# An LSTM, an attention, a GRU and a mixture of experts on one core: both recurrences in one loop, the GRU 29 steps behind

## The chip, the core and the metric

The kernel runs on one core of a Trainium2 chip. The metric is the device time of one execution in microseconds; three executions of the kernel before took 735.74 us in the median (731.89 to 736.39). The engines are TensorE (PE, with PEld for its loads of the stationary operand), VectorE (DVE), ScalarE (ACT), GpSimd (POOL) and SyncE (SP). Each works through its own instructions in order and waits for the others at semaphores.

## What is computed

x has 16 sequences (b) of 128 steps (t) with 128 features (d), all in float32. Four stages follow each other:

```python
# LSTM over t, its hidden state starting at cond_1024
a = xw_t + prev_h @ Wh
i, f, o = sigmoid(a[:, :128]), sigmoid(a[:, 128:256]), sigmoid(a[:, 256:384]); g = tanh(a[:, 384:])
next_c = f * prev_c + i * g
next_h = o * tanh(next_c)
# causal attention over the LSTM's outputs: 16 heads, keys and values from a latent of 32
x = x + attention(lstm_out)
# GRU over t on the new x
z, r = sigmoid(comb @ Wz + bz), sigmoid(comb @ Wr + br)
h_cand = tanh(concat(x_t, r * h) @ Wh + bh)
h_new = (1.0 - z) * h + z * h_cand
h_next = where(prop, tanh(h_new @ Wp + bp), h_new)      # prop: after each 4th step
# 8 experts of 128 -> 512 -> 128 with gelu, the best 2 of each token weighted
x = x + experts(gru_out)
```

The GRU's step t needs the attention's output for step t, and that needs the LSTM's steps 0 to t. The experts need the GRU's outputs, token by token.

## The kernel before

A step of either recurrence is a chain over three engines. The state is kept as two float16 parts (`hhi` and `hlo`, `ghi` and `glo`), each product with a weight is taken as high by high, high by low and low by high, and sigmoids are written as tanh. An LSTM step: 12 matmuls with 16 columns (8 on `hhi`, 4 on `hlo`), one tanh over the four gates (`lT`, line 729), on DVE `lP`, `oK` and the new cell in `lT`, a tanh of the cell (`lC`, line 733), on DVE `hhi`, `hfull` and `hlo` (lines 906 to 909). A GRU step: 6 such matmuls (or 2 in float32 on `gp` at the first of each four steps), a tanh of both gates (`gT`, line 770), on DVE `gRZ` and `gA`, a float32 matmul on `gRZ`, a tanh (`gC`, line 777), on DVE `gB`, `ghi`, `g8` and `glo`; after each fourth step a matmul with `gWp` and a tanh give `gp`.

The program has three stages, one behind the other.

1. The LSTM in loops over groups of 8 steps (`GS`). Four such groups make a block of `TB` = 32 steps; while the LSTM does block p, the attention of block p-1 is placed between its steps: one unit (one sequence, 16 heads x 32 queries) at steps 1 to 4 of a group for the scores, 3 to 6 for the transposes of the probabilities, 5 to 7 for the values. `keep_warm` puts matmuls of 512 columns on zeros between steps.
2. `last_attention`: the 16 units of the last block, with no recurrence beside them.
3. The GRU in a loop of 16 turns of 8 steps; beside each step one expert on the 128 tokens of the turn before (`layer1`, `layer2`), and the routing (18 small DVE operations, `routing`) spread over the turn.

A float32 matmul appears in the trace as two passes. POOL clears buffers, splits the experts' first weights `w1` into two float16 parts (lines 318 to 321, once, over all 4096 columns), and copies each unit's queries into the block-diagonal `qbd` (line 345).

## Time and profile before

| | |
|---|---|
| time, median of 3 runs | 735.74 us (731.89 to 736.39) |
| the profiled execution, first to last instruction | 731.8 us |
| busy: PE, PEld | 685.2 us (94%), 598.1 us (82%) |
| busy: DVE, ACT, POOL | 461.2 us (63%), 361.6 us (49%), 113.7 us (16%) |
| first LSTM tanh | 28.8 us |
| LSTM's loop | to 330 us |
| last attention | to 381 us |
| GRU's loop | 384 to 711 us |
| rest of the experts | to 731.8 us |

Matmuls are pipelined, so PE counts as busy over more than the time that it takes up: what a matmul costs is the distance from its start to the next one's. A wait printed behind an instruction is idle time of its engine just before it, and the arrow names what ended it.

### The profile page before, as it was taken

The numbers are of one execution on the slowest core, as the hardware profiler recorded it, in microseconds if no ns is written. First come the engines' busy times: TensorE is split into PE (matmuls) and PEld (weight loads), VectorE is DVE, ScalarE is ACT, GpSimd is POOL, SyncE is SP. The second block draws the span as 40 slices with busy tenths as digits, with TensorE's granted clock in tenths as the row PEclk, the third lists the DMA queues.
The fourth block names the chain that finished last, engine by engine and source line by source line (L and its number), as shares of the span: only waits on it lengthen the run. The fifth ranks groups of instructions, "written<-read, shape, count | busy, mean of one in ns | idle before, by whom it ended". The sixth has DMA issues, their size and how long they took to land.

```text
span 731.8 us, 22615 instructions
## 1 busy us (share of the span) xinstructions
PE 685.2 (94%) x7655; PEld 598.1 (82%) x7655; DVE 461.2 (63%) x2374; ACT 361.6 (49%) x1317; POOL 113.7 (16%) x291
## 2 busy tenths in 40 slices
PE   6942999999999999998999999999999999999998
PEld 4521557988888888887989999999999999999996
DVE  2379446676777777876876555655556555565553
ACT  2210224343444444445556666666666666666665
POOL 3068003221322132213310000000000000000000
PEclk8775899898999999999999999999999999999999
DMA  8320000000000000000000000000000000000000
GB/s 196 140 92 0 1 0 3 1 1 0 1 2 0 0 3 2 0 0 1 1 0 6 6 4 0 4 4 4 4 4 4 4 4 3 0 4 4 4 4 8
DMA packets 5669, 9.45 MB, mean 13 GB/s; under 512 B 1884, under 2 KB 4724, under 8 KB 5120
## 3 DMA queue, kind: packets, MB, share of 16 engines
q1 hardware_dynamic: 5008, 6.59, 2.8%
q10 hardware_dynamic: 624, 2.38, 1.3%
q8 instruction: 21, 0.34, 0.2%
q14 instruction: 16, 0.13, 0.1%
HBM read 7.78 MB, written 1.18 MB: 12 GB/s over the span
## 4 chain that ended last, share of the span: by engine, by line
PE 85%; DVE 9%; ACT 2%; issue 2%; DMA 1%; ACTq 0%; POOL 0%; DVEq 0%; POOLq 0%
PE p L363 60%; PE pL L363 21%; PE p L455 4%; DVE hhi L906 4%; DMA Wout<-in_Wout 1%; DVE On L874 1%; DVE lP L897 1%; DVE mx L860 1%; ACT lC L733 1%; ACT lT L729 1%; DVE OT L881 1%; DVE P L865 0%; DVE oK L898 0%; PE p L559 0%; DVE hlo L909 0%
## 5 line engine op out<-in xcount | busy, mean ns | idle before, releaser
L363 PE MATMUL p<-w,hidA 128*128 128x128 f32 x548 | 122.0, 308 | 0.0
L363 PE MATMUL p<-ghi,w1lo 128*128 128x128 f16 x544 | 105.0, 219 | 0.0
L363 PE MATMUL p<-glo,w1hi 128*128 128x128 f16 x544 | 104.8, 219 | 0.0
L363 PE MATMUL p<-ghi,w1hi 128*128 128x128 f16 x544 | 104.8, 218 | 0.0
L761 ACT ACTIVATE hidA<-p,b 128x128 f32<-128x128 f32 x272 | 85.2, 364 | 32.9 <-PE p L363 32.9
L363 PE MATMUL p<-w,hidB 128*128 128x128 f32 x548 | 91.8, 290 | 0.1
L363 PEld LDWEIGHTS p<-w,hidA 128*128 128x128 f32 x548 | 82.7, 192 | 7.8 <-issue 7.7
L761 ACT ACTIVATE hidB<-p,b 128x128 f32<-128x128 f32 x274 | 85.1, 366 | 2.1 <-PE p L363 2.1
L729 ACT ACTIVATE lT<-pL 128x64 f32<-128x64 f32 x128 | 28.5, 223 | 107.7 <-PE pL L363 106.5
L345 POOL COPY qbd<-qT 32x128 f32 x216 | 62.9, 291 | 69.4 <-PE p L363 58.6
L1016 DVE SCALAR_TENSOR_TENSOR gRZ<-gT,g 128x32 f32<-128x32 f32 x128 | 24.7, 193 | 77.4 <-ACT gT L770 74.4
L363 PE MATMUL p<-latT,qbd 128*128 (+1 forms) x512 | 73.3, 288 | 0.0
L363 PEld LDWEIGHTS pL<-hhi,lWhi 128*128 128x128 f16 x512 | 36.4, 98 | 44.0 <-DVE hhi L906 42.4
L363 PEld LDWEIGHTS p<-w,hidB 128*128 128x128 f32 x548 | 72.0, 192 | 0.3 <-ACT hidB L761 0.3
L363 PE MATMUL p<-latN,PTs 32*128 (+4 forms) x512 | 67.7, 276 | 0.8
L363 PE MATMUL pL<-hhi,lWhi 128*128 128x16 f16 x512 | 42.1, 172 | 26.8 <-DVE hhi L906 25.9
L363 PE MATMUL p<-still 128*128 128x512 bf16 x209 | 63.5, 416 | 2.9 <-DVE hlo L819 2.1
L363 PEld LDWEIGHTS p<-latT,qbd 128*128 128x128 f32 x512 | 64.3, 197 | 1.0 <-issue 0.2
L363 PEld LDWEIGHTS p<-latN,PTs 32*128 32x128 f32 (+3 forms) x512 | 61.0, 189 | 2.2 <-issue 1.0
L906 DVE TENSOR_TENSOR hhi<-oK,lC 128x16 f16<-128x16 f32 x128 | 46.3, 362 | 22.5 <-ACT lC L733 21.2
L733 ACT ACTIVATE lC<-lT 128x16 f32<-128x16 f32 x128 | 27.6, 216 | 63.4 <-DVE lT L900 63.1
L363 PEld LDWEIGHTS p<-ghi,w1hi 128*128 128x128 f16 x544 | 55.7, 102 | 1.0
(179 smaller groups left out, 1546.9 us busy)
## 6 DMA issues: line engine op xcount, KB each, us to landing
w<-in_w SPq DMA_DIRECT2D x2, 2048.0 KB, 10.2
out<-acc SPq DMA_DIRECT2D x18, 64.0 KB, 1.5
xT<-in_xT ACTq DMA_DIRECT2D x1, 1024.0 KB, 12.0
...
```

What stands on the lines that cost most here:

```text
L345: pool.tensor_copy(qbd[r, k % 2, :, q, :], qT[r, j % 2, :, ds(b0 + k, 1), :] .rearrange("p g o t -> p g (o t)")).then_inc(qbd_done, 1)
L363: return nc.tensor.matmul(out, lhsT=lhsT, rhs=rhs, start=start, stop=stop, skip_group_check=True)
L455: last = nc.tensor.transpose(pT[:, 128 * g:128 * (g + 1)], P[:, k, g, :], ident[:, :])
L729: A(lT[:, 0:4, :], pL[hf][:, :, s, :], ACT.Tanh, scale=1.0 / SP).then_inc(l_tanh, 1)
L733: A(lC[:, :], lT[:, 4, :], ACT.Tanh, scale=0.5).then_inc(l_tc, 1)
L761: last = A(hid[:, c, :], bank[:, TOK * c:TOK * (c + 1)], ACT.Gelu, bias=b1[:, e, 2 * half + c:2 * half + c + 1], scale=1.0 / SP)
L860: V.tensor_reduce(mx[:, k % 2, :], S_of(k, L), AX.X, ALU.max).then_inc(mx_done, 1)
L874: V.tensor_tensor(On[:, :, :], O_of(k)[:, :, 0:LD], rs[:, :].unsqueeze(2).to_broadcast([128, HG, LD]), ALU.mult).then_inc(on_done, 1)
L881: V.transpose(OT[:, :, k, :], On[:, :, :]).then_inc(ot_done, 1)
L897: V.scalar_tensor_tensor(lP[:, :, :], lT[:, 0:2, :], 1.0, lT[:, 3:5, :], ALU.add, ALU.mult).then_inc(l_mul, 1)
L906: V.tensor_tensor(hhi[:, slot, :], oK[:, :], lC[:, :], ALU.mult).then_inc(l_hi, 1)
L1016: V.scalar_tensor_tensor(gRZ[:, :, :], gT[:, :, :], 1.0, g8[:, at:last + 1:last - at, :], ALU.add, ALU.mult).then_inc(g_rh, 1)
```

## The change

- One straight-line program of 166 steps k takes the place of the three stages. Step k does the LSTM's step t = k (while t < 128), the GRU's step g = k - `LAG` = k - 29, a piece of the attention and a piece of the experts. All loops are gone from the code; waits are for constants.
- The attention works in blocks of `TB` = 16 queries and in units of two sequences (4 x 128 rows of scores in one bank): 8 units a block. In each 16 steps the scores stand at k mod 16 = 2 to 9, the transposes at 3 to 10, the values at 4 to 11, one unit a step. Scores are three float16 products of 16 x (block + 1) keys instead of one float32 product of 128 columns. The projections stand at k mod 16 = 9 and 12, so that the GRU's first step of a block may follow at 13. The last 8 steps of each 16 hold no scores.
- The experts run once for a block of 256 tokens instead of twice for 128. `up_at` puts an expert's two halves (6 matmuls with 256 columns each) at k mod 16 = 13 (4 halves), 14 (2), 15 (4), 0 (2) and 1 (4); `down_at` puts one product of 128 tokens at each step, a block later. The last block's experts follow the last GRU step at k = 157 to 165.
- Routing is done twice in 16 steps (k mod 16 = 5 and 13) in one go: 6 DVE operations (`route_first`) at the end of the step, 2 on POOL (`rank_experts`), one tanh on ACT, 10 on DVE (`route_rest`) at the end of the next step.
- All hidden states and x with the attention added (`x1T`, `hhi`, `hlo`, `g8`, `ghi`, `glo`) stay in full length on chip; `stx` and its copies on POOL are gone.
- Banks: one for the LSTM's gates, one for the GRU's, one for scores and latents (`pS`), one for transposes and values (`pV`), one for queries, projections and routing (`pC`), two for the experts' first products (`pH`), one for their second (`pY`).
- POOL gets more to do: each of 64 units has its queries spread by 4 copies of 32 x 256 float16 (before: 216 copies of 32 x 128 float32 on POOL, 40 on ACT); the latents are split into two float16 parts (2 operations each 8 steps); it scales and splits the GRU's weights, `b2` and `w1`, the last in 12 operations of 1024 columns placed at k = 28 to 31.
- `keep_warm` remains in front of the loop (20) and in steps 0 and 3 to 17 (4 each).

```diff
-TB = 32
+TB = 16
+LAG = 29
+O_S, O_T, O_V = 2, 3, 4
+O_P = (9, 12)
+O_R = (5, 13)
+E_STEP = (0, 0, 1, 2, 2, 3, 4, 4)
...
+            def turn_probs(n):
+                pe.wait_ge(exp_done, n + 1)
+                if n:
+                    pe.wait_ge(on_done, n)
+                for j in range(4):
+                    last = nc.tensor.transpose(pV[:, 128 * j:128 * (j + 1)], P[:, n % 3, j, :], ident[:, :])
+                last.then_inc(pt_mm, 1)
...
+                if n >= 2:
+                    pe.wait_ge(gelu, 2 * (n - 1))
...
+            for k in range(STEPS):
+                t, g = k, k - LAG
+                ups, downs = up_at(k), down_at(k)
+                if 0 <= g < T:
+                    g_step(g)
+                if t < T:
+                    l_step(t)
+                if unit_at(k, O_V) is not None:
+                    values(unit_at(k, O_V))
+                elif half_at(k) is None and ups:
+                    expert_up(*ups.pop(0))
+                if half_at(k) is not None:
+                    project(half_at(k), k)
+                if 0 <= g < T:
+                    g_candidate(g)
+                if k % GS == 0 and GS <= k <= T:
+                    lat_q(k // GS - 1, k)
+                if unit_at(k, O_S) is not None:
+                    scores(unit_at(k, O_S), k)
+                while ups or downs:
+                    if downs:
+                        expert_down(*downs.pop(0))
+                    if ups:
+                        expert_up(*ups.pop(0))
+                if unit_at(k, O_T) is not None:
+                    turn_probs(unit_at(k, O_T))
+                if route_at(k) is not None:
+                    route_x(*route_at(k), k)
...
+                if t % GS == GS - 1 and t + 1 < T:
+                    l_fill((t + 1) // GS)
+                if (g + 1) % GS == 0 and 0 <= g + 1 < T:
+                    g_fill((g + 1) // GS)
+                if 0 <= g < T - 1 and g % 4 == 3:
+                    g_propagate(g)
```

DVE's order in a step is: `gRZ`, `gA`, `lP`, `oK`, `lT`; the normalisation of a unit; `gB`, `ghi`, `g8`; `hhi`, `hfull`; `glo`; `hlo`; then what no recurrence waits for directly: adding x, latents, maximum and subtraction of a unit, `route_rest`, `combine`, `turn_values`, `route_first`. ACT's order is `gT`, `lT`, the unit's exp, the first gelu of a step with ups, `gC`, `lC`, the query copy, the other gelus, the copy of the transposes (`pt_copy`), the routing's tanh, `gp`.

The places in the programs. On PE, in the step behind the LSTM's and GRU's own matmuls, a step of before in the GRU's loop (`w1hi`, `w1lo` are the first expert weights, `hidA` and `hidB` the halves of the hidden layer, `gRZ` the candidate's input):

```order
L363 MATMUL pL<-glo,gWhi 128x16 x2
L363 MATMUL p<-ghi,w1hi 128x128
L363 MATMUL p<-glo,w1hi 128x128
L363 MATMUL p<-ghi,w1lo 128x128
L363 MATMUL p<-ghi,w1hi 128x128
L363 MATMUL p<-glo,w1hi 128x128
L363 MATMUL p<-ghi,w1lo 128x128
L363 MATMUL p<-b2P,ones 128x512
L363 MATMUL p<-w,hidA 128x128
L363 MATMUL pL<-gRZ,gW 128x16
```

And of the change, the step k = 52, from the LSTM's last matmuls to the scores (`PTs` the turned probabilities, `latN` the values, `qbd` the queries):

```order
L444 MATMUL pL<-hlo,lWhi 128x16 x4
L444 MATMUL pV<-latN,PTs 128x33 x4
L444 MATMUL pG<-gRZ,gW 128x16
L444 MATMUL pS<-cmask,ident 128x4x16
L444 MATMUL pS<-lathi,qbd 128x48
L444 MATMUL pS<-latlo,qbd 128x48
```

The same step's end:

```order
L444 MATMUL pY<-b2P,onesP 128x128
L444 MATMUL pY<-w,hid 128x128 x4
L539 MATMUL pV<-ident,P 128x128 x4
L444 MATMUL pG<-ind,biasP 128x512
L444 MATMUL pG<-x1T,gWx 128x128 x3
L444 MATMUL pG<-g,gWp 128x16
L444 MATMUL pG<-g,gW 128x16 x2
```

The values now stand ahead of the candidate's matmul, and the transposes, on which ACT's copy and the next step's values wait, are at the end of the step, behind a product of the experts.

On ACT, around an expert step of before (`hidA`, `hidB`: gelu):

```order
L770 ACTIVATE gT<-pL 128x32
L761 ACTIVATE hidB<-p,b 128x128 x2
L777 ACTIVATE gC<-pL 128x16
L758 REGISTER_ALU
L761 ACTIVATE hidA<-p,b 128x128 x2
```

And of the change, at k = 45, the first step with ups (`th` is the routing's tanh):

```order
L753 ACTIVATE gT<-pG 128x32
L756 ACTIVATE lT<-pL 128x64
L745 ACT_TABLE_LOAD
L745 ACTIVATE hid<-pH,b 128x256 x2
L763 ACTIVATE gC<-pG 128x16
L766 ACTIVATE lC<-lT 128x16
L745 ACTIVATE hid<-pH,b 128x256 x6
L777 ACTIVATE th<-low 128x8
L753 ACTIVATE gT<-pG 128x32
```

A table load now stands between the gates' tanh and the candidate's, and the routing's tanh stands ahead of the next step's `gT`. ACT had 2 table loads in all, one at its first instruction and one ahead of the GRU's loop; it has 14, one at the start and then one ahead of the first gelu and one ahead of the first exp of nearly every 16 steps.

On POOL, the split of `w1` before:

```order
L318 TENSOR_SCALAR w1hi<-w 128x4096
L319 TENSOR_SCALAR w<-w 128x4096
L321 TENSOR_TENSOR w1lo<-w,w1hi 128x4096
```

And of the change, behind the first block's queries:

```order
L413 COPY qbd<-qh 32x8x32 x32
L398 CAST lathi<-latT 128x16x8
L400 TENSOR_TENSOR latlo<-latT,lathi 128x16x8
L390 TENSOR_SCALAR w1hi<-w 128x1024
L391 TENSOR_SCALAR w<-w 128x1024
L393 TENSOR_TENSOR w1lo<-w,w1hi 128x1024
```

It comes four times, in quarters, in front of the queries of the second block.

## Rows read from the trace of the kernel before

**Rows 1.** The page's head and its chain that ended last, by engine.
```profile
span 731.8 us, 22615 instructions
PE 85%; DVE 9%; ACT 2%; issue 2%; DMA 1%; ACTq 0%; POOL 0%; DVEq 0%; POOLq 0%
```
**Rows 2.** Stretches: us, PE, PEld, DVE, ACT, POOL busy (x instructions), granted clock, DMA share, GB/s.
```profile
42.00:71.30 29.30, 6.23 (x49) 3.44 (x47) 27.49 (x15) 1.65 (x6) 28.98 (x3) 0.57 0.00 0
132.00:134.00 2.00, 2.00 (x19) 1.30 (x18) 0.92 (x5) 0.68 (x2) 0.28 (x1) 0.50 0.00 0
113.00:330.00 217.00, 211.85 (x2570) 190.36 (x2568) 160.38 (x843) 96.42 (x323) 55.90 (x192) 0.97 0.00 1
332.00:381.00 49.00, 45.88 (x399) 43.26 (x399) 36.78 (x90) 28.89 (x59) 16.10 (x56) 1.00 0.00 1
384.00:711.00 327.00, 327.00 (x3772) 300.96 (x3772) 193.58 (x1185) 202.64 (x816) 5.37 (x16) 1.00 0.01 4
```
**Rows 3.** Timeline of PEld (start us, us) in one GRU step: distances between loads.
```profile
592.73 0.10 PEld L363 LDWEIGHTS p<-glo,w1hi 128*128 128x128 f16 x1
592.79 0.10 PEld L363 LDWEIGHTS p<-ghi,w1lo 128*128 128x128 f16 x1
...
593.01 0.53 PEld L363 LDWEIGHTS p<-w,hidB 128*128 128x128 f32 x4
593.46 0.10 PEld L363 LDWEIGHTS pL<-ghi,gWhi 128*128 128x128 f16 x1
...
593.60 0.10 PEld L363 LDWEIGHTS pL<-ghi,gWhi 128*128 128x128 f16 x1
593.62 0.10 PEld L363 LDWEIGHTS pL<-ghi,gWlo 128*128 128x128 f16 x1
```
**Rows 4.** Timeline of one LSTM step without attention.
```profile
33.40 0.17 DVE L906 TENSOR_TENSOR hhi<-oK,lC 128x16 f16<-128x16 f32 x1 [0.28 <-ACT lC L733]
34.22 0.22 ACT L729 ACTIVATE lT<-pL 128x64 f32<-128x64 f32 x1 [0.86 <-PE pL L363]
35.16 0.18 DVE L906 TENSOR_TENSOR hhi<-oK,lC 128x16 f16<-128x16 f32 x1 [0.28 <-ACT lC L733]
```
**Rows 5.** Timeline of one GRU step, gate tanh to gate tanh.
```profile
593.90 0.20 ACT L770 ACTIVATE gT<-pL 128x32 f32<-128x32 f32 x1 [0.28 <-PE pL L363]
594.81 0.18 ACT L777 ACTIVATE gC<-pL 128x16 f32<-128x16 f32 x1
595.53 0.17 DVE L1034 TENSOR_TENSOR glo<-g,ghi 128x16 f16<-128x16 f32 x1
596.10 0.20 ACT L770 ACTIVATE gT<-pL 128x32 f32<-128x32 f32 x1 [0.28 <-PE pL L363]
```
**Rows 6.** Groups by line and shape: xcount | busy us, mean ns | idle before, releaser.
```profile
L676 ACT ACTIVATE PTs<-p 128x512 f32<-128x512 f32 x16 | 9.6, 597 | 11.2 <-PE p L455 11.2
L761 ACT ACTIVATE hidA<-p,b 128x128 f32<-128x128 f32 x272 | 85.2, 364 | 32.9 <-PE p L363 32.9
L363 PE MATMUL p<-latT,qbd 128*128 x480 | 69.0, 288 | 0.0
L860 DVE TENSOR_REDUCE mx<-p 128x4 f32<-128x512 f32 x16 | 10.9, 681 | 4.8 <-PE p L363 3.9
L907 DVE TENSOR_TENSOR hfull<-oK,lC 128x16 f32<-128x16 f32 x128 | 22.2, 174 | 0.0
L345 POOL COPY qbd<-qT 32x128 f32 x216 | 62.9, 291 | 69.4 <-PE p L363 58.6
```
**Rows 7.** Timelines of DVE and POOL at the split of `w1`.
```profile
42.21 8.78 DVE L906 TENSOR_TENSOR hhi<-oK,lC 128x16 f16<-128x16 f32 x1 [0.28 <-ACT lC L733]
42.15 10.54 POOL L318 TENSOR_SCALAR w1hi<-w 128x4096 f16<-128x4096 f32 x1 [34.40 <-DMA w<-in_w]
```
**Rows 8.** Timeline of ACT at its second table load.
```profile
378.88 0.60 ACT L676 ACTIVATE PTs<-p 128x512 f32<-128x512 f32 x1 [0.84 <-PE p L455]
379.49 1.28 ACT L785 ACT_TABLE_LOAD   x1
380.79 0.21 ACT L785 ACTIVATE th<-still 128x8 f32<-128x8 bf16 x1
```

More of the change, by code:

```diff
@@ L24, with unit_at, half_at, route_at @@
 SP = SH * SW
+LAG = 29
+O_S, O_T, O_V = 2, 3, 4
+O_P = (9, 12)
+O_R = (5, 13)
+LAST = T + LAG
+E_STEP = (0, 0, 1, 2, 2, 3, 4, 4)
+NHID = 8
+def unit_at(k, o):
+    q, u = divmod(k - o, TB)
+    return NU * (q - 1) + u if u < NU and 1 <= q <= NBLK else None
+def half_at(k):
+    for h, o in enumerate(O_P):
+        q, r = divmod(k - o, TB)
+        if r == 0 and 1 <= q <= NBLK:
+            return 2 * (q - 1) + h
+    return None
+def route_at(k):
+    for tg, o in enumerate(O_R):
+        q, r = divmod(k - o, TB)
+        if r == 0 and 2 <= q <= NBLK + 1:
+            return q - 2, tg
+    return None
+def up_at(k):
+    out = []
+    for m in range(NBLK):
+        for e in range(E):
+            at = LAST + e if m == NBLK - 1 else TB * m + LAG + TB + E_STEP[e]
+            if at == k:
+                out += [(m, e, 0), (m, e, 1)]
+    return out
+def down_at(k):
+    out = []
+    for m in range(NBLK):
+        for e in range(E):
+            for tg in range(2):
+                at = LAST + 1 + e if m == NBLK - 1 else TB * m + LAG + TB + 2 + 2 * e + tg
+                if at == k:
+                    out.append((m, e, tg))
+    return out
+STEPS = LAST + 1 + E
 def build(nc, a, out):
@@ L349, in stage @@
[L349 to L357 removed]
+            pool.memset(whole(bias), 0.0).then_inc(cleared, 1)
+            pool.memset(whole(gscale), 0.0).then_inc(cleared, 1)
@@ new lines, in bank_c, with before_c @@
+            def bank_c(nq, npj, nr):
+                if nq:
+                    pe.wait_ge(q_lo, 4 * nq)
+                if npj:
+                    pe.wait_ge(x1_done, npj)
+                if nr:
+                    pe.wait_ge(r_copy, 2 * nr)
+            def before_c(k):
+                nq = len([j for j in range(k) if j % GS == 0 and GS <= j <= T])
+                npj = len([j for j in range(k) if half_at(j) is not None])
+                nr = len([j for j in range(k) if route_at(j) is not None])
+                bank_c(nq, npj, nr)
@@ new lines, in l_step @@
+            def l_step(t):
+                s = t % GS
+                if t:
+                    pe.wait_ge(l_hi, t)
+                for g in range(4):
+                    mm(pL[:, g, s, :], lWhi[:, g, :], hhi[:, t, :])
+                    mm(pL[:, g, s, :], lWlo[:, g, :], hhi[:, t, :])
+                if t:
+                    pe.wait_ge(l_lo, t)
+                for g in range(4):
+                    last = mm(pL[:, g, s, :], lWhi[:, g, :], hlo[:, t, :])
+                last.then_inc(l_gates, 1)
@@ new lines, in g_step @@
+            def g_step(t):
+                s = t % GS
+                if t % 4 == 0:
+                    pe.wait_ge(g_p, t // 4 + 1)
+                    for g in range(2):
+                        last = mm(pG[:, g, s, :], gW1[:, g, :], gp)
+                else:
+                    pe.wait_ge(g_hi, t)
+                    for g in range(2):
+                        mm(pG[:, g, s, :], gWhi[:, g, :], ghi[:, t - 1, :])
+                        mm(pG[:, g, s, :], gWlo[:, g, :], ghi[:, t - 1, :])
+                    pe.wait_ge(g_lo, t)
+                    for g in range(2):
+                        last = mm(pG[:, g, s, :], gWhi[:, g, :], glo[:, t - 1, :])
+                last.then_inc(g_rz, 1)
@@ L1038, in _ @@
[L1038 to L1042 removed]
+                V.tensor_scalar(bias[:, n, :], bias[:, n, :], gscale[:, n:n + 1], None, ALU.mult).then_inc(set_bias, 1)
+            dve.wait_ge(set_bias, 2)
+            V.tensor_copy(whole(biasP), whole(bias)).then_inc(set_bias, 1)
+            dve.wait_ge(set_bias, 3)
```

1397 lines of the change are left out of this document (621 added, 776 removed).

## The prediction

> **What bounds the kernel now.** I read the page's head and its chain first: 731.8 us, and of the chain that ended last TensorE holds 85% [rows 1]. The stretches [rows 2] say what that is made of. In the GRU's loop (384 to 711) PE is busy all the time and 128 steps take 327 us, 2.55 us each. In the LSTM's loop with attention (113 to 330) 96 steps take 217 us, 2.26 each, PE busy 98%, DVE 74%. The last attention takes 49 us with no recurrence beside it. Between 42.0 and 71.3 PE is nearly idle: POOL works 28.98 us on three instructions, and DVE's `hhi`, normally 0.17, takes 8.78 [rows 4, 7].
>
> Busy is not used up, so I price matmuls by distances between loads [rows 3]: 0.06 us (0.055) for float16 with 128 columns, 0.45 / 4 = 0.11 for a float32 pass of 128 columns or fewer, 0.025 for float16 with 16 columns. The chains: an LSTM step alone is 35.16 - 33.40 = 1.76 us [rows 4]; a GRU step is 2.2 us [rows 5], gate tanh to candidate tanh 0.91, candidate to `glo` 0.72, `glo` to gate tanh 0.57. By distances, 8 GRU steps of before hold about 18 us of matmuls in 20.4: 88% used.
>
> **PE's work after.** I count 16 steps of the full program (k = 45 to 128). Float16 of 16 columns: 12 x 16 + 6 x 12 = 264, 6.6 us. Float32 on 16 columns: 16 candidates, 8 on `gp`, 4 with `gWp`, 56 passes, 6.2. Experts up: 96 matmuls of 256 columns; not in the trace, twice 0.055, 10.6. Experts down: 128 passes and 16 bias rows, 15.0. Values 64 passes, 7.0; transposes 32, 3.5; scores 96 float16 of 16 to 128 columns, 0.025 to 0.055 each, 3.8; latents and queries 30 x 0.055, 1.7; projections 16 passes, 1.8; fills 4.0; routing 0.7. Sum 61 us, 3.8 per step. The same stages in before need 2.55 + 2.26 + 49/128 = 5.2 us per step. In the matmuls themselves only the scores get cheaper: 512 float32 passes (480 of one form in [rows 6]) at 0.11 are 56 us, the new ones 30 over the whole kernel.
>
> **What is added in waits.** Both chains now pass through each engine in one order, so a wait of one holds the other. I took each of the 16 steps through PE, ACT and DVE with the distances above. With nothing else a step with both chains takes about 2.3 us, and at each fourth one the `gp` path adds 0.45 of waiting. The terms in 16 steps, beyond the 61:
> - the copy of the transposes (0.6 us, [rows 6]) starts when PE's step ends and the next step's values need it: 0.42 us at 5 unit steps, 2.1;
> - `gp`: 4 x 0.45, 1.8;
> - routing: `th` waits for six DVE operations behind PE's last matmul and stands ahead of the next `gT`, about 1.2 us; then ten more DVE operations of 0.2 delay the next `gRZ`: twice in 16 steps, 3.5;
> - ups: a gelu of 256 columns (two of 0.364 at 128 columns are issued 0.31 apart, [rows 6]; I take 0.42 each, 0.83 for a half) is longer than the half's 0.66 of PE, and with two banks the fourth half of a step waits for it: 3.0;
> - steps too light for both chains (k mod 16 = 2, 3, 10, 11): 2.5;
> - table loads: 379.49 to 380.79 [rows 8], 1.3 us each, two in 16 steps, in front of `gC`; half is hidden behind PE's work, 1.4.
>
> Together 14.3: 75 us for 16 steps, 4.7 per step, PE used 81%. DVE comes next: 13 operations of 0.17 in the two chains of a step (2.2 us), behind them a unit's maximum (0.68 over 512 columns, [rows 6]) and a subtraction like it. That tail falls into PE's work and ends, at 128 keys, about 1.0 us into the next step, just in time.
>
> Of the table the trace shows 1.3 us for a switch. The Trainium skill (ScalarE: Activation LUTs, What ACT_TABLE_LOAD costs) gives 2.66 us with a drain; the rows show no such drain, and by it the sum would be 13 x 1.35 = 18 us more.
>
> **The sum**, in order of k:
> - to the first LSTM tanh 17 (before 28.8): the fold of the attention's weights and 15 warming matmuls no longer stand ahead of it, and what it waits for is `lWx` behind other loads. Bounds 13 and 22.
> - k = 0 to 2: 12, three steps of 1.8 and the fold, now inside.
> - k = 3 to 15: 13 x 1.8 and 8 for POOL's operations on `b2` and the GRU's weights: 31.
> - k = 16 to 28: ten steps of 2.4 with a unit, three of 1.9: 30; and `w1`: 12 quarters with the same 29 us of POOL in all. Between quarters DVE gets one burst through, so about two quarters pass per step: 18 (bounds 8 and 29; before it cost 29.3 - 3 x 1.76 = 24).
> - k = 29 to 44, both recurrences and units, no experts: 6 x 2.5 + 10 x 3.8 + 2 = 55.
> - k = 45 to 128: 84 x 4.7 = 395.
> - k = 129 to 156, no LSTM, attention until 139: 11 x 4.2, 5 x 4.7 with ups, 11 x 2.4, and the first: 100.
> - k = 157 to the end, last experts: 8 x 3.4, edges and the store: 33.
> - clock: in k = 26 to 33 and 146 to 156 PE has less than 60% to do, and before it was granted 0.50 at places (132 to 134, PE's busy 2.00 of 2.00) [rows 2]; 6.
>
> 17 + 12 + 31 + 48 + 55 + 395 + 100 + 33 + 6 = 697. The shown median is 3.9 above the profiled span and the lowest run equals it; I add 1: **698 us**, 38 less than the median.
>
> **The rivals.**
> - *PE close to its work.* If the waits overlap better than my one-step-at-a-time count (the six terms are not all on one path), a full step takes 4.1: 84 x 0.6 = 50 less, 648 us. For it: 88% used in the GRU's loop of before. Against: there was one chain there and no unit. Chance 0.18.
> - *POOL holds DVE (slower).* In [rows 7] an instruction of DVE with two inputs in SBUF stood still for 8.8 us while POOL read SBUF. 256 copies of 32 x 256 (by [rows 6] 0.29 us at 128 elements, about 0.45 here) and 32 splits of latents are 128 us of POOL reading beside both chains, 11 of DVE's operations per step having two such inputs. For it: the copies stand in the same steps as the units. Against: with 216 short copies in before `hfull`, of two inputs, has a mean of 174 ns, that of an undisturbed one [rows 6]. I count 1 us in 16 steps as nothing. If each copy costs the chain its whole 0.45, 115 us come on top: 810; from 0.15 us per copy on (38 / 256) nothing is gained. Chance 0.14, at about 765. The Trainium skill (SBUF — State Buffer, Who interferes with whom) has the rule: the two share a port pair, one blocks the other for the whole instruction; by it the copies would block. The trace agrees for the long operations and not visibly for the short ones.
> - *The clock.* Where PE waits more often, the granted clock falls to 0.50 and the 3.8 us of a step become up to 7.6. If that happens in a fifth of the 84 steps: 17 x (7.7 - 4.7) = 51, 749 us. For it: 0.50 in stretches of before with attention and LSTM, which were about 83% used. Against: 1.00 in all of 384 to 711. Chance 0.12.
> - My forecast, with its own range 665 to 735: 0.56.
>
> **Numbers.** Faster by over 1% (about what a measurement here can tell from no change) means below 728: nearly all of the first rival and 0.52 of the forecast, 0.70. Within 1%: the forecast's edge and the lower ends of the two slower ones, 0.08. Slower: 0.22. The range 640 to 762 leaves out the far end of POOL's case and a still better overlap, 0.2 in all.
>
> **What would show it.** Right: about 4.7 us from one `lT` to the next in k = 45 to 128, PE's granted clock 1.00 there; `PTs` late before the values; `th` waiting for `low` over 1 us; 13 further table loads of 1.3. Wrong: `hhi`, `ghi`, `gRZ` with means far over 0.18 us outside k = 25 to 31 (POOL); clock under 0.9 in full steps; PE idle over 1 us per step for one releaser not named above; or a first tanh past 22 us.

## The result, and the profile after

The changed kernel takes **744.56 us** in the median of 20 runs (738.29 to 751.22). The kernel before, measured beside it, takes 736.18 (729.99 to 741.70). The ratio is 1.0112 with a 95% interval of 1.0083 to 1.0141: the change makes the kernel 1.1% slower. The forecast was 698. Over the 20 runs the time follows TensorE's mean granted clock: the shortest has 0.877, the longest 0.849.

The page of the changed kernel: head, busy shares, two of its rows in 40 slices (busy tenths of PE, granted clock in tenths), and the chain that ended last.

```profile
span 744.1 us, 18666 instructions
PE 623.6 (84%) x6863; PEld 564.0 (76%) x6898; DVE 430.7 (58%) x2359; ACT 282.3 (38%) x983; POOL 174.9 (24%) x364
...
PE   5968865998888888888898889988998788877898
...
PEclk8777565555899999999999999999999999995599
...
PE 63%; DVE 18%; ACT 10%; issue 6%; DMA 1%; POOL 1%; SPq 0%; DVEq 0%; POOLq 0%
```

PE has 62 us less to do than before (685.2), and the chain's share of PE went from 85% [rows 1] to 63%: that part of the change works. But the granted clock is 0.5 or 0.6 in slices 5 to 10 and 0.5 in slices 37 and 38; in the page of before it is 0.8 or more in all slices behind the fourth.

ScalarE's timeline of the changed kernel gives the marks between the stages. `lT` is the LSTM's gate tanh, `gT` the GRU's; the rows are the steps k = 16, 20, 21, 29, 45, 129, 141 and 156.

```profile
58.29 0.23 ACT L756 ACTIVATE lT<-pL 128x64 f32<-128x64 f32 x1 [1.36 <-PE pL L444]
67.11 0.22 ACT L756 ACTIVATE lT<-pL 128x64 f32<-128x64 f32 x1
71.39 0.22 ACT L756 ACTIVATE lT<-pL 128x64 f32<-128x64 f32 x1
109.77 0.20 ACT L753 ACTIVATE gT<-pG 128x32 f32<-128x32 f32 x1 [5.96 <-PE pG L444]
185.13 0.20 ACT L753 ACTIVATE gT<-pG 128x32 f32<-128x32 f32 x1 [1.12 <-PE pG L444]
588.58 0.20 ACT L753 ACTIVATE gT<-pG 128x32 f32<-128x32 f32 x1 [0.71 <-PE pG L444]
643.44 0.20 ACT L753 ACTIVATE gT<-pG 128x32 f32<-128x32 f32 x1 [0.71 <-PE pG L444]
705.32 0.20 ACT L753 ACTIVATE gT<-pG 128x32 f32<-128x32 f32 x1 [1.88 <-PE pG L444]
```

Its stretches between such marks (us, then busy us of PE, PEld, DVE, ACT, POOL with their instructions, granted clock, DMA share, GB/s):

```profile
58.30:109.80 51.50, 40.06 (x424) 36.49 (x425) 31.02 (x131) 12.39 (x46) 33.40 (x44) 0.62 0.00 1
110.10:142.90 32.80, 22.59 (x245) 20.59 (x247) 23.30 (x112) 8.21 (x39) 19.53 (x27) 0.50 0.01 1
142.90:185.10 42.20, 37.13 (x349) 35.94 (x351) 24.07 (x150) 10.47 (x47) 6.12 (x16) 0.54 0.01 2
185.10:588.60 403.50, 351.99 (x4378) 327.49 (x4395) 259.87 (x1530) 187.67 (x653) 80.06 (x208) 0.96 0.01 3
667.30:705.30 38.00, 30.46 (x179) 28.85 (x180) 14.58 (x86) 4.32 (x24) 0.64 (x2) 0.52 0.00 1
```

The 84 steps with everything in them (185.1 to 588.6) take 403.5 us, 4.80 each, at a mean clock of 0.96. The same work before took 2.55 + 2.26 + 49 / 128 = 5.19 per step [rows 2], so the loop does win 33 us there. They are lost, and more, where one part of the program is missing: at k = 16 to 28 (51.5 us, clock 0.62), k = 29 to 44 (75.4 us, 0.50 and 0.54) and k = 146 to 155 (38 us, 0.52).

The 0.96 is a mean too. Taken step by step, from one `gT` to the next, 76 of the 84 steps ran at 1.00 and eight at 0.60 to 0.77 (k = 45, 55, 71, 86, 102, 105, 118, 121). The step k = 105 in the changed kernel and, with the same instructions, in h_warm2_w1 (an experiment below):

```profile
472.64:479.04 6.40, 6.31 (x73) 6.20 (x69) 3.82 (x19) 1.61 (x6) 0.00 (x0) 0.73 0.01 3
```

```profile
460.88:465.67 4.79, 4.70 (x73) 4.59 (x69) 3.34 (x18) 1.61 (x6) 0.00 (x0) 1.00 0.00 0
```

PE is busy for nearly the whole step in both; at the lower clock the step is 1.61 us longer.

Against the sum of the prediction, stage by stage, from such marks. The last three columns are kernels of the experiments below; the forecast's 100 and 33 are shown with their border at k = 156 instead of 157, one step of 2.4 us.

| steps | forecast | changed kernel | g_warm2 | h_warm2_w1 | l_all |
|---|---|---|---|---|---|
| to k = 3 | 29 | 27.1 | 29.4 | 26.8 | 30.0 |
| k = 3 to 15 | 31 | 31.2 | 31.2 | 31.0 | 27.2 |
| k = 16 to 28 | 48 | 51.5 | 45.0 | 49.1 | 39.9 |
| k = 29 to 44 | 55 | 75.4 | 66.1 | 61.7 | 61.4 |
| k = 45 to 128 | 395 | 403.5 | 403.8 | 404.8 | 408.0 |
| k = 129 to 155 | 97.6 | 116.7 | 110.8 | 109.5 | 109.7 |
| k = 156 to the end | 35.4 | 38.8 | 38.0 | 38.0 | 40.0 |
| clock | 6 | in the stages | | | |
| sum | 697 | 744.1 | 724.3 | 720.8 | 716.2 |

What half the clock does is seen in PE's timeline of the changed kernel (with DVE's `ghi` put in), one GRU step with an expert's product beside it, at k = 154, and the same in g_warm2, where the clock is 1.00. Lines between those shown are left out.

```profile
696.24 0.61 PE L444 MATMUL pG<-gRZ,gW 128*128 128x16 f32 x2 [0.51 <-DVE gRZ L933]
696.75 2.02 PE L444 MATMUL pY<-w,hid 128*128 128x128 f32 x8
697.31 0.17 DVE L949 SCALAR_TENSOR_TENSOR ghi<-gA,gB 128x16 f16<-128x16 f32 x1
698.56 0.22 PE L444 MATMUL pG<-ghi,gWhi 128*128 128x16 f16 x1
...
699.43 0.61 PE L444 MATMUL pG<-gRZ,gW 128*128 128x16 f32 x2 [0.51 <-DVE gRZ L933]
```

```profile
683.88 0.40 PE L444 MATMUL pG<-gRZ,gW 128*128 128x16 f32 x2 [0.51 <-DVE gRZ L939]
684.18 1.11 PE L444 MATMUL pY<-w,hid 128*128 128x128 f32 x8
685.12 1.03 PE L444 MATMUL pS<-still 128*128 128x512 bf16 x4
685.99 0.17 PE L444 MATMUL pG<-ghi,gWhi 128*128 128x16 f16 x1
```

Eight float32 passes take 698.56 - 696.75 = 1.81 us at 0.50 and 685.12 - 684.18 = 0.94 at 1.00. The GRU's next matmuls are queued behind them. At half the clock the product outlasts the chain beside it: `ghi` is done at 697.48, and `gC` to the end of `glo` is 0.9 us (696.88 to 697.78), but TensorE takes `ghi` up only at 698.56. So TensorE, with little to do, becomes what the recurrence waits for: 3.19 us a step from `gRZ` to `gRZ` here (699.43 - 696.24).

### The profile page after: what moved, and what is told of

The parts are those of the page before. It is cut to its first block, busy times and chain, and to the rows that moved or that the text cites. A ratio compares the mean times of both kernels' runs of the same rounds, so it can differ in the third digit from the quotient of the medians.

```text
span 744.1 us, 18666 instructions
## 1 busy us (share of the span) xinstructions
PE 623.6 (84%) x6863; PEld 564.0 (76%) x6898; DVE 430.7 (58%) x2359; ACT 282.3 (38%) x983; POOL 174.9 (24%) x364
## 4 chain that ended last, share of the span: by engine, by line
PE 63%; DVE 18%; ACT 10%; issue 6%; DMA 1%; POOL 1%; SPq 0%; DVEq 0%; POOLq 0%
PE pY L444 17%; PE pG L444 11%; PE pH L444 10%; PE pV L444 9%; PE pL L444 5%; PE pV L539 4%; PE pC L444 4%; PE pS L444 3%; ACT hid L745 3%; ACT PTs L735 3%; DVE hhi L953 1%; DMA lWx<-in_lWx 1%; DVE ghi L949 1%; DVE gB L946 1%; DVE acc L924 1%
## 5 line engine op out<-in xcount | busy, mean ns | idle before, releaser
L444 PE MATMUL pY<-w,hid 128*128 128x128 f32 x1024 | 158.6, 304 | 0.0
L444 PEld LDWEIGHTS pY<-w,hid 128*128 128x128 f32 x1024 | 139.6, 212 | 0.1
L413 POOL COPY qbd<-qh 32x256 f16<-32x256 f16 x256 | 101.7, 397 | 137.9 <-PE pS L444 124.1
L745 ACT ACTIVATE hid<-pH,b 128x256 f32<-128x256 f32 x256 | 105.6, 471 | 62.5 <-PE pH L444 61.3
L444 PE MATMUL pV<-latN,PTs 128*128 128x33 f32 x512 | 79.4, 304 | 9.2 <-ACT PTs L735 9.0
L444 PE MATMUL pG<-gRZ,gW 128*128 128x16 f32 x256 | 53.3, 285 | 36.6 <-DVE gRZ L933 36.5
L444 PEld LDWEIGHTS pV<-latN,PTs 128*128 128x128 f32 x512 | 72.6, 219 | 12.7 <-ACT PTs L735 12.0
L444 PE MATMUL pH<-ghi,w1hi 128*128 128x256 f16 x256 | 71.0, 277 | 6.4 <-ACT hid L745 5.4
L444 PE MATMUL pH<-ghi,w1lo 128*128 128x256 f16 x256 | 71.2, 278 | 0.0
L444 PE MATMUL pH<-glo,w1hi 128*128 128x256 f16 x256 | 71.2, 278 | 0.0
L924 DVE SCALAR_TENSOR_TENSOR acc<-pY,gates,acc 128x128 f32<-128x128 f32 x128 | 44.4, 347 | 36.1 <-PE pY L444 35.4
L763 ACT ACTIVATE gC<-pG 128x16 f32<-128x16 f32 x128 | 23.3, 182 | 87.8 <-PE pG L444 87.6
```

Of the source, the lines that this page charges most:

```text
L413: pool.tensor_copy(qbd[r, n % 2, :, :, q, :], qh[r, p % 2, :, 2 * u:2 * u + 2, :, :].rearrange("p l b (g c) t -> p l (b g) (c t)", g=2)).t ...
L444: return nc.tensor.matmul(o, lhsT=lhsT, rhs=rhs, start=start, stop=stop, skip_group_check=True)
L745: A(hid[:, e % NHID, 2 * cp + c, :], pH[cp][:, 256 * c:256 * (c + 1)], ACT.Gelu, bias=b1[:, e, 2 * cp + c:2 * cp + c + 1], scale=1.0 / SP) ...
L763: A(gC[:, :], pG[:, 2, g % GS, :], ACT.Tanh, scale=1.0 / SP).then_inc(g_c, 1)
L924: V.scalar_tensor_tensor(acc[:, m % 3, tg, :], pY[:, D * tg:D * (tg + 1)], gates[:, m % 2, tg, e:e + 1], acc[:, m % 3, tg, :], ALU.mult, A ...
```

## The experiments

All are compared with runs of the kernel before on the same chip. Times are medians; stage times are those of the profiled execution. Differences to the changed kernel are between medians measured at different times, and not on one chip, so those under some 4 us are not read. Where steps of two kernels are compared, each is a stretch from one `gT` to the next, and its clock is that of the stretch; "at a clock of 1.00" are those of 0.99 and 1.00. The code shown is shortened.

### Four parts of the sum, one each

**a_warm**: keeps the clock up with matmuls on zeros.

```diff
                 if k < 18:
                     keep_warm(0 if k in (1, 2) else 4)
+                elif k < 45:
+                    keep_warm(1 if k < 28 else 2 if unit_at(k, O_T) is not None else 5)
+                elif k > 140 and k < LAST:
+                    keep_warm(2, pS)
```

> The changed kernel (744.56 us) with warming matmuls of 512 columns on zeros added at the end of light steps: 1 a step at k = 18 to 27, 5 at k = 28 to 44 where no unit is turned and 2 where one is, 2 at k = 141 to 156. Theory (the half clock of 70 to 190 us and of 665 to 705 us is what my sum missed): granted clock 0.95 or more in those stretches, unit steps at k = 20 to 27 from 4.4 to about 2.8 us, k = 29 to 45 from 75 to about 58, k = 146 to 157 from 3.2 to 2.4 a step; in all about 36 us less, 708. Rival (the low clock only mirrors waits on DVE, POOL and ACT, and costs little by itself): the clock rises and the time stays above 735.

Measured: 738.63 us (729.41 to 742.77, 4 runs), beside 735.99 of before; the profiled execution has a span of 733.9. The program has 103 matmuls on zeros more. Of the profile, the stretches 67 to 79 us, k = 29 to 44, and k = 146 to 155:

```profile
67.00:79.00 12.00, 11.00 (x101) 10.04 (x102) 6.40 (x31) 3.02 (x12) 4.72 (x13) 0.50 0.00 1
108.70:180.10 71.40, 63.44 (x664) 50.21 (x661) 44.69 (x261) 19.97 (x88) 26.85 (x43) 0.76 0.01 2
663.00:696.40 33.40, 26.03 (x200) 21.63 (x200) 14.76 (x86) 4.26 (x25) 0.64 (x2) 0.85 0.00 1
```

The clock came back in part only: one extra matmul a step does not hold it at k = 20 to 22, where PE is busy 11.00 of 12.00 us and still at 0.50. So the experiment did not reach what it was to test; the gain of about 6 us fits a clock that rose in part, but four runs that lie 13 us apart do not fix its size.

**b_w1**: `w1` is split by ScalarE and DVE, one expert a step at k = 26 to 33.

```diff
-                if 28 <= k < 32:
-                    split_w1(k - 28)                       # POOL, 3 x 1024 columns
+                if 26 <= k < 26 + E:                       # ACT, behind lC
+                    A(w1hi[:, k - 26, :], w1[:, k - 26, :], ACT.Copy, scale=SW).then_inc(set_w1h, 1)
+                if 26 <= k < 26 + E:                       # DVE, behind hlo
+                    V.scalar_tensor_tensor(w1lo[:, e, :], w1[:, e, :], SW, w1hi[:, e, :], ALU.mult, ALU.subtract)
```

> The split of w1 taken off POOL: ACT writes w1hi and DVE w1lo, one expert (512 columns) a step at k = 26 to 33; nothing else. Theory (POOL's twelve operations hold DVE from 90 to 121 us, 8 steps in 36 us): about 17 us less, 727; if the clock also stays up, a few more. Rival (those steps are slow because of the half clock, POOL's operations are covered): no more than 4 us less, 740 or above.

Measured: 739.26 us (730.80 to 747.11, 10 runs), ratio to before 1.0012 (0.9967 to 1.0058). About 5 us less than the changed kernel, where 727 was expected. The profiled execution is one of the longest (746.3), so only its parts can be read: k = 24 to 28 shrinks from 23.3 to 19.5 us and k = 29 to 44 from 75.4 to 72.4, while the full steps take 409.4 instead of 403.5, ten of them at a low clock instead of eight. At k = 29 to 44 its clock is 0.52, as in the changed kernel: taking POOL's split away did not bring it back.

**c_probs**: `turn_probs` ahead of the experts' products instead of behind them.

```diff
+                if unit_at(k, O_T) is not None:
+                    turn_probs(unit_at(k, O_T))
                 while ups or downs:
...
-                if unit_at(k, O_T) is not None:
-                    turn_probs(unit_at(k, O_T))
```

> The transposes of the probabilities moved ahead of the experts' second product in each step, so that ACT's copy of 0.6 us is done when the next step's values want it. Theory (0.35 to 0.42 us of PE waiting in five unit steps of 16, 8 blocks): 14 us less, 730, and PE's wait on PTs (21 us in the changed kernel) near 0. Rival (another chain, the candidate's, is as late): PTs' wait goes but the wait for gRZ grows by as much, 741 or above.

Measured: 747.36 us (743.68 to 749.61, 4 runs), ratio 1.0147 (1.0076 to 1.0218). No gain: the wait moves. Two groups of the waits between 185 and 590 us (who waited for whom: us in total, times, longest), in the changed kernel and then in c_probs:

```profile
ACT PTs L735 <- PE pV L539: 71.0, 40, 3.3
...
ACT gT L753 <- PE pG L444: 34.0, 44, 1.5
```

```profile
ACT gT L753 <- PE pG L444: 55.1, 60, 3.6
...
ACT PTs L735 <- PE pV L539: 36.0, 40, 1.3
```

ScalarE gets the transposes earlier (71 to 36 us of waiting for them) and then waits longer for the gates of the next step (34 to 55): the experts' product, now behind the transposes, is what TensorE does last. Its full steps take 410.6 us instead of 403.5, but the 74 of them at a clock of 1.00 are together only 1.5 us shorter than the same steps elsewhere; the order gained next to nothing, and the difference lies in ten steps at a low clock.

**d_pool2**: each of POOL's 256 copies into `qbd` is done twice, first into a tile that nobody reads.

```diff
+                    pool.tensor_copy(qbx[r, n % 2, :, :, q, :],
+                                     qh[r, p % 2, :, 2 * u:2 * u + 2, :, :].rearrange(...))
                     pool.tensor_copy(qbd[r, n % 2, :, :, q, :],
```

> Each of POOL's 256 copies of queries done twice, the first time into a tile that nobody reads: 102 us more of POOL reading SBUF beside both chains. If POOL's reading holds DVE's operations of two inputs (the slower rival of the prediction), 60 to 100 us more, 805 to 845, and means of hfull, ghi, gB over 250 ns. If short copies hold little, under 10 us more, at most 755; scores would then wait for POOL only where its two copies (3.5 us a unit) are longer than a step.

Measured: 757.12 us (749.55 to 759.89, 4 runs), ratio 1.0309 (1.0235 to 1.0383): 12.6 us more in the medians, 0.05 per copy. The two profiled executions are only 3.6 us apart (747.7 and 744.1), and d_pool2's 74 full steps at a clock of 1.00 are together 2.8 us longer than the same steps without the copies; how much of the 12.6 is the clock's isn't known. DVE's busy time between 110 and 588 us, in the changed kernel and then in d_pool2:

```profile
110.00:588.00 478.00, 307.34 (x1791) 0.89 0.01 3
```

```profile
110.00:588.00 478.00, 316.76 (x1786) 0.90 0.01 3
```

9.4 us for the 192 copies that are added there, 0.05 each out of 0.4 (five of DVE's instructions fall outside the second window, so it is a little more): short copies on POOL make DVE busy for about an eighth of their time longer. The rival in which they hold it for all of it (115 us in the prediction) is ruled out, and so is its decision point of 0.15 us per copy.

### The clock, warmed harder, and two waits taken away

**g_warm2**: as a_warm, with more.

```diff
-                if k < 18:
-                    keep_warm(0 if k in (1, 2) else 4)
+                if k < 29:
+                    keep_warm(0 if k in (1, 2) else 4 if unit_at(k, O_T) is None else 3)
+                elif k < 45:
+                    keep_warm(6 if unit_at(k, O_T) is None else 3)
+                elif k > 144 and k < LAST:
+                    keep_warm(4, pS)
```

> More warming matmuls than in a_warm (512 columns on zeros, at the end of a step's TensorE work): 4 and 3 (with a unit) at k = 16 to 28, 6 and 3 at k = 29 to 44, 4 at k = 145 to 156. Theory half clock (what k = 16 to 44 and 129 to 156 take beyond the forecast is TensorE at 1.2 GHz): the granted clock is 0.95 or more in 60 to 185 and after 670, k = 29 to 44 takes 62 us (75.4 in the changed kernel, 71.4 in a_warm), k = 129 to 156 takes 106 (118), and the span is 715 to 722. Rival, the steps there are long for waits between engines whatever the clock: the clock comes back and k = 29 to 44 stays at 70 or more.

Measured: 728.82 us (726.13 to 737.30, 10 runs) beside 735.09 of before, ratio 0.9932 (0.9895 to 0.9968); span 724.3. Its stretches for the unit step k = 20, for k = 29 to 44 in two parts, and for k = 146 to 155:

```profile
69.30:72.50 3.20, 2.82 (x43) 2.39 (x42) 2.34 (x12) 1.29 (x5) 2.56 (x7) 1.00 0.01 3
105.70:138.60 32.90, 28.61 (x325) 20.37 (x323) 26.49 (x128) 9.92 (x45) 21.44 (x31) 0.91 0.01 1
138.60:171.70 33.10, 29.46 (x350) 24.03 (x349) 21.00 (x134) 10.16 (x43) 4.70 (x13) 0.92 0.01 2
653.40:686.30 32.90, 26.44 (x220) 20.52 (x220) 14.69 (x86) 4.28 (x23) 0.64 (x2) 1.00 0.01 1
```

With 156 more matmuls of 512 columns the program is 15.7 us shorter. Three stages gain, those that I named: 51.5 to 45.0, 75.4 to 66.1, 116.7 to 110.8, together 21.7 us; the full steps stay at 403.8. The unit step at k = 20 goes from 4.28 us (71.39 - 67.11) at 0.50 to 3.17 at 1.00. The expected 62 us for k = 29 to 44 was not reached, nor was 106 for k = 129 to 156 or a span of 715 to 722.

**h_warm2_w1**: g_warm2 and b_w1 together.

> The warming of g_warm2 and the split of w1 off POOL (as in b_w1) together. Theory half clock: the two gains add, k = 24 to 28 takes 17 us (23.3), k = 29 to 44 56 to 60 us (75.4), near the forecast's 55, and the whole is 705 to 712. If the idle time behind POOL's split isn't what lowers the clock, it is no better than g_warm2 less 4 us.

Measured: 721.58 us (717.11 to 722.59, 4 runs), ratio 0.9787 (0.9720 to 0.9855). It is 7.2 us beyond g_warm2, so the two gains add, but the expected 705 to 712 was missed. Here k = 29 to 44 takes 61.7 us, and k = 24 to 28 takes 17.3 as expected. What is missing lies before them, in the stretch k = 20 to 23:

```profile
67.36:89.62 22.26, 20.93 (x171) 17.01 (x171) 8.46 (x44) 4.83 (x18) 6.56 (x17) 0.52 0.01 1
```

The program up to k = 25 is that of g_warm2, with the same matmuls on zeros, and there the clock was 1.00: k = 16 to 23 took 22.6 us, here 31.9. The added matmuls did not hold the clock each time, and where it was 0.50 they cost more than they gave: a unit step took 5.11 us, against 4.28 without them. The term of the prediction for `w1` stood wholly in k = 16 to 28; in the changed kernel POOL's split ran from 90.3 to 121.1 us, the last third of it beside both recurrences.

**e_notable**: Tanh in place of the experts' Gelu (the function computed is another one), so that no table is loaded in the loop.

```diff
-                    A(hid[:, e % NHID, 2 * cp + c, :], pH[cp][:, 256 * c:256 * (c + 1)], ACT.Gelu,
+                    A(hid[:, e % NHID, 2 * cp + c, :], pH[cp][:, 256 * c:256 * (c + 1)], ACT.Tanh,
```

> The experts' Gelu is a Tanh with the same bias and scale, so its output differs; ScalarE has no table to load for it. Prices the switches between Gelu's table and Tanh's. Theory of the sum: 1.3 us each, half hidden, about 2 in 16 steps, 13 in all: 8 to 17 us less than the changed kernel (728 to 736). Rival, they stand wholly before gC or the next gT and hold both chains, or cost a drain besides: over 25 us less.

Measured: 745.68 us (743.27 to 747.99, 4 runs), ratio 1.0142 (1.0073 to 1.0212). Nothing is gained, neither the 8 to 17 us of my term nor the rival's 25; the 76 full steps at a clock of 1.00 are together 0.8 us shorter than the same steps with the loads. In the changed kernel one such load reads, in ScalarE's timeline:

```profile
338.13 1.28 ACT L745 ACT_TABLE_LOAD   x1
339.43 0.84 ACT L745 ACTIVATE hid<-pH,b 128x256 f32<-128x256 f32 x2
340.16 0.18 ACT L763 ACTIVATE gC<-pG 128x16 f32<-128x16 f32 x1
```

It does stand between `lT` and `gC`. But in such a step PE works through the experts' products up to the next `gT`'s matmuls anyway, and the load's 1.28 us are covered by them. The row agrees with the first one seen [rows 8], and no drain shows; the Trainium skill (ScalarE: Activation LUTs, What ACT_TABLE_LOAD costs) gives 2.66 us with a drain, which neither kernel bears out.

**f_th**: ScalarE's routing tanh a step later.

```diff
                     A(lC[:, :], lT[:, 4, :], ACT.Tanh, scale=0.5).then_inc(l_tc, 1)
+                if route_at(k - 1) is not None:
+                    A(th[:, :], low[:, :], ACT.Tanh, scale=0.5).then_inc(r_th, 1)
...
-                if route_at(k) is not None:
-                    A(th[:, :], low[:, :], ACT.Tanh, scale=0.5).then_inc(r_th, 1)
```

> ScalarE does routing's tanh (th) one step later, behind the next step's gT, lT, gC and lC, so it no longer holds them; DVE's ten operations stay in the same step but start later. Theory of the sum: th costs 1.2 us of 16 steps' two routings each, so 2.4 per 16 steps, 16 to 20 us over the run: 727. Rival, the operations on DVE behind it carry the cost, later too: same as the changed kernel within 4 us, or slower, since glo's neighbours now wait behind th.

Measured: 742.72 us (736.75 to 745.63, 4 runs), ratio 1.0108 (1.0042 to 1.0173). The full steps take 403.5 us, as in the changed kernel; at a clock of 1.00 the steps k mod 16 = 5 are 6.4 us shorter in sum and those behind them, 6 and 7, 6.8 longer. The rival holds.

### What a microsecond of TensorE is worth, and the other half of the comparison

**j_more** and **k_less**: one matmul of 256 columns more, or one less, in each chunk of the experts' first layer (in k_less the product of `w1lo` and `ghi` is left out).

```diff
                     mm(Y, w1hi[:, e, cols], lo)
-                    last = mm(Y, w1lo[:, e, cols], hi)
+                    mm(Y, w1lo[:, e, cols], hi)                              # j_more
+                    last = mm(Y, still[:, 0:128], still[:, 0:2 * TOK])
...
-                    mm(Y, w1hi[:, e, cols], lo)
-                    last = mm(Y, w1lo[:, e, cols], hi)
+                    last = mm(Y, w1hi[:, e, cols], lo)                       # k_less
```

> The changed kernel with one more matmul of 256 columns (zeros, 0.11 us) per expert, half and chunk: 32 more in 16 steps, 3.5 us of TensorE, 18.5 us in k = 45 to 128 and about 22 by the end. Theory, TensorE's work is on the path in full steps and the waits are beside it in series: all of it shows, k = 61 to 124 takes 14 us more (307 before) and the run 20 or more. Rival, the waits between engines set the pace and TensorE has room in them: under a third of it, 7 us or less on the run.

> The changed kernel without the third matmul of the experts' first layer (w1lo times ghi; the output loses that correction): 32 matmuls of 0.11 us less in 16 steps. Theory, TensorE's work is on the path: 3.5 us less in 16 steps, 14 in k = 61 to 124, the run 20 less, unless the granted clock falls for it. Rival, waits set the pace (ScalarE's gelu is then what the halves wait for): 5 us less or nothing.

Measured: 762.02 us (758.69 to 763.10, 6 runs) and 743.62 us (739.14 to 744.78, 6 runs); ratios 1.0353 (1.0301 to 1.0405) and 1.0101 (1.0051 to 1.0151). The four times 16 steps from k = 61, first in the changed kernel:

```profile
261.50:337.60 76.10, 65.64 (x846) 61.40 (x848) 49.24 (x293) 34.42 (x123) 15.42 (x40) 0.98 0.01 4
337.60:412.70 75.10, 66.02 (x847) 61.88 (x848) 50.13 (x293) 34.74 (x122) 15.39 (x40) 0.98 0.01 4
...
sum 307.10, PE 269.24 PEld 252.48 DVE 202.14 ACT 139.91 POOL 61.59; mean PE 67.31 PEld 63.12 DVE 50.53 ACT 34.98 POOL 15.40
```

In j_more:

```profile
sum 315.90, PE 280.93 PEld 263.57 DVE 200.37 ACT 140.72 POOL 61.73; mean PE 70.23 PEld 65.89 DVE 50.09 ACT 35.18 POOL 15.43
```

In k_less:

```profile
262.90:337.30 74.40, 62.07 (x813) 58.15 (x814) 49.24 (x293) 34.17 (x123) 15.50 (x40) 0.98 0.01 3
337.30:415.80 78.50, 68.20 (x816) 64.51 (x817) 50.09 (x293) 34.56 (x123) 15.46 (x40) 0.89 0.01 4
415.80:491.90 76.10, 63.62 (x814) 59.64 (x815) 51.47 (x293) 34.94 (x123) 15.45 (x40) 0.98 0.01 4
491.90:567.00 75.10, 65.38 (x815) 61.02 (x817) 51.25 (x293) 35.39 (x123) 15.48 (x40) 0.95 0.01 3
```

14 us of TensorE more cost 8.8 us (63%). The same less gives 1.7 + 1.7 + 3.0 = 6.4 of 10.5 us (61%) in the three turns where the clock is about as before, and in the fourth, where it is 0.89, 3.4 us are given back. These turns still differ in their clock. In single steps at 1.00, which agree to 0.01 us from turn to turn, the five steps with ups are 2.2 us longer in j_more (63% of 3.5) and 1.7 us shorter in k_less (49%). So neither expectation held as written: five to six tenths of TensorE's work lie on the path in full steps, the rest in its waits. In k_less 13 of the 84 steps ran at a low clock, against 7 to 10 in five executions with the changed kernel's own steps, and its six runs had a mean clock of 0.845 to 0.853, against 0.870 to 0.874 in j_more's: less work went with a lower clock, and the run gained nothing.

**i_before_w1**: the kernel before, with the one edit that has nothing to do with the loop.

```diff
-            pool.tensor_scalar(whole(w1hi), whole(w1), SW, None, ALU.mult).then_inc(w1_split, 1)
-            pool.tensor_scalar(whole(w1), whole(w1), SW, None, ALU.mult).then_inc(w1_split, 1)
-            pool.tensor_tensor(whole(w1lo), whole(w1), whole(w1hi), ALU.subtract).then_inc(w1_split, 1)
...
                     if first:                              # ACT, last_attention, k = 0 to 3
                         gru_weights(k)
+                        A(w1hi[:, 2 * k:2 * k + 2, :], w1[:, 2 * k:2 * k + 2, :], ACT.Copy, scale=SW)
...
+                    if first:                              # DVE, last_attention
+                        V.scalar_tensor_tensor(w1lo[:, 2 * k:2 * k + 2, :], w1[...], SW, w1hi[...], ALU.mult, ALU.subtract)
```

> The kernel before, with w1's split taken off POOL's start: ScalarE and DVE do it in four parts in the first turn of the last attention (332 to 345 us), where no recurrence runs. Theory: DVE no longer stands still between 42 and 71, 24 us less, and the last attention hides most of the 4 + 4 us: 712 to 718. Then what the changed kernel gains with the same split moved (b_w1, h_warm2_w1) is nothing that the single loop is needed for. Rival: the stall of DVE there is not POOL's; then it stays near 735.

Measured: **711.30 us** (707.32 to 711.87, 4 runs) beside 736.98, ratio 0.9641 (0.9586 to 0.9696): 25.7 us less. Its stretch where the split stood:

```profile
42.00:71.30 29.30, 26.98 (x312) 15.77 (x318) 14.43 (x101) 8.71 (x36) 0.00 (x0) 1.00 0.00 1
```

PE does 312 matmuls where it did 49 [rows 2], at a clock of 1.00 instead of 0.57, and from the LSTM's last `hhi` to the GRU's first `gT` it takes 55.8 us (306.35 to 362.11) instead of 53.7 (330.44 to 384.13). Moving three operations gives more than the whole change with all that was mended in it.

**l_all**: h_warm2_w1, f_th, and `b2` split by ScalarE and DVE at k = 12 to 14 instead of by POOL.

```diff
+                if 12 <= k < 15:                           # ACT; r = all, from 64, from 96
+                    A(b2P[r, :], b2[r, :], ACT.Copy).then_inc(set_b2, 1)
+                if 12 <= k < 14:                           # DVE; r = from 64, from 96
+                    V.tensor_tensor(b2[r, :], b2[r, :], b2P[r, :], ALU.subtract).then_inc(set_b2, 1)
```

> h_warm2_w1 with routing's tanh one step later (f_th) and the split of b2 moved off POOL onto ScalarE and DVE at k = 12 to 14. Expected by the parts: b2 5 us in k = 3 to 15 (31.2 in the changed kernel, of it about 8 for POOL's operations), the tanh 2: 713 to 717. Rival: the b2 stall only moves, and f_th's gain was the clock's: 721, as h_warm2_w1.

Measured: 717.64 us (713.18 to 718.30, 4 runs), ratio 0.9727 (0.9669 to 0.9785), 6.3 us more than i_before_w1 on the same chip. Its stretches k = 16 to 28 and 45 to 128:

```profile
57.20:97.10 39.90, 34.53 (x455) 27.89 (x460) 26.64 (x134) 14.37 (x48) 14.16 (x36) 1.00 0.01 2
158.50:566.50 408.00, 353.85 (x4376) 329.89 (x4393) 259.88 (x1530) 187.14 (x652) 82.05 (x208) 0.96 0.01 3
```

From k = 16 to 155 the mean clock of each stage is 0.96 or more (0.97 at k = 29 to 44, 0.98 at k = 129 to 155), though ten of the full steps ran at 0.95 or less and took part in the 408.0 us. `b2` gave 4.0 us in k = 3 to 15 (31.2 to 27.2).

## Why the prediction was wrong

The step that failed is the clock's term: 6 us in the sum, at least 21.7 measured by g_warm2, about 8 more in the full steps, and by an estimate some 36 in all. The price of a full step, 4.7 us, is what the rows show at a full clock.

Point by point, in the order of its sum:

- **To k = 15**: 60 forecast, 58.3 measured. Right, with the attention's fold inside the first steps.
- **k = 16 to 28**: 48 against 51.5, but not by its terms. A unit step was to take 2.4 us. It takes 4.28 at half clock and 3.17 at full clock with three warming matmuls of 0.21 in it, so by estimate about 2.5 without, if each costs its length there as it does at k = 154.
- **k = 29 to 44, the first stage that failed**: 55 against 75.4. Of the 20, 9.3 are the clock's (g_warm2), 4.4 are POOL's split of `w1` that ran on into this stage (h_warm2_w1 less g_warm2, the clock's rise from 0.92 to 0.97 included), and 6.7 remain at a clock of 0.97, with 72 matmuls on zeros among them: units without experts were priced at 3.8.
- **k = 45 to 128**: 395 against 403.5, 4.7 a step against 4.80, and the difference is the clock's. For each step I took its time at a clock of 1.00 in an execution with the same instructions; the steps k mod 16 = 6 and 7, of which one ran at a low clock in nearly every pair, were taken as the shortest pair on record. That adds up to 395.7 us, 4.71 a step, 7.8 less than the changed kernel took. So the price of a step is right; its parts are not confirmed. The terms for the routing's tanh and the table loads gave nothing when they were taken away (f_th, e_notable), nor did the order of the transposes (c_probs). j_more and k_less show why such a list cannot be added: work and waits overlap by four to five tenths. (A reading of mine was off without harm: two gelus of 128 columns start 0.26 us apart in the trace of before, not 0.31; a half takes 0.84 us, priced at 0.83.)
- **k = 129 to 156, the second stage that failed**: 100 against about 120 (116.7 to k = 156, and one step). The stretch to k = 141 takes 54.9 against some 50, the five steps with ups 23.9 against 23.5, and the last eleven 41 against 26.4 at a clock of 0.52; a plain step there takes 3.19. In f_th and j_more, which add no matmuls on zeros, the clock was still 1.00 at k = 147, and the same step took 2.11 and 2.10, less than the forecast's 2.4; in j_more:

```profile
685.37:687.47 2.10, 1.59 (x17) 1.48 (x17) 1.23 (x8) 0.38 (x2) 0.00 (x0) 1.00 0.00 0
```

  Warming costs too: with two matmuls a step it is 2.49 (a_warm), with four 2.92 (685.99 less 683.07, where the step before begins).
- **The clock, the mis-sized term**: 6 us in the sum, 21.7 measured (the three stages of g_warm2, net of what warming itself costs), and 7.8 in the full steps. The prediction named the right steps (k = 26 to 33, 146 to 156) but read "PE has less than 60% to do" as a small loss. What the rows show is that the clock fell earlier (0.50 already at k = 20) and stayed down while PE was busy, in a_warm 11 of 12 us: the work at half speed fills the time that full speed would leave idle. As a rival the clock was to fall in a fifth of the full steps; it fell in eight of 84, in part of each. Why in these and, in another execution of the same steps, in others is not shown.
- **POOL, the rival**: not so. The medians of DVE's operations are what they were, apart from the splits of `w1` and `b2`. Here the changed kernel, by tile and shape, ns min/median/max:

```profile
L946 DVE TENSOR_TENSOR gB<-gRZ,gC x128: 163/176/1737, 111.1 to 706.7; 128x16 f32<-128x16 f32 x128
L954 DVE TENSOR_TENSOR hfull<-oK,lC x128: 159/168/380, 19.5 to 580.0; 128x16 f32<-128x16 f32 x128
```

  The medians are those of before (176, and 168 for `hfull`); the 1737 is the split of `w1`. The Trainium skill (SBUF — State Buffer, Who interferes with whom) calls the port pair that the two share an exclusive lock, and says of DVE's two-port modes that whoever issues first holds it for the whole instruction. That fits the long operations nearly (8.78 of 10.54 us in [rows 7]) and not the short copies (0.05 of 0.4 us in d_pool2).
- **PE close to its work (648)**: not so. 16 full steps take 75.1 to 78.1 us, not 66; PE is busy 67.3 of 76.8 us in the mean, and at the full clock the steps come to 4.71 us, not 4.1; by j_more and k_less its work is only in part what sets the pace.

In sum 697 + 15.7 (the clock, 21.7 for 6) + 4.4 (`w1` in the next stage) + 8.5 (full steps) + 6.7 (k = 29 to 44 at a clock of 0.97) + 13.2 (k = 129 to 155 with g_warm2's clock) + 3.4 (the end) - 1.7 - 3.0 (to k = 15, and k = 16 to 28 with that clock) = 744.2, against 744.1 profiled. Of the 8.5, 7.8 are the clock's by the steps above. Of the 13.2 some 7 are g_warm2's own matmuls (0.8 us in each of k = 146, 147, 148 and 150, none at 149, taken as nine steps of 0.8), which in the changed kernel are the clock's. With these the clock's part is by estimate 21.7 + 7.8 + 7, some 36 us. The rest of the 6.7 and 13.2 is not pinned to a wait by an experiment: it is only the difference between my price of a step and the marks.

Beside the terms, one thing was missing from the argument: the gain was measured against a kernel that loses 25.7 us to one POOL stretch, which the prediction itself had priced at 24. By the profiled executions the 84 full steps save 33 us (436 of 731.8 in before, 403.5 now), and everything outside them takes 340.6 us where it took 296.
